# x added by ScalarE and GpSimd, token statistics in the third step, block projection and selection moved, in an attention and GRU kernel

## What is computed

```python
# x: (128, 32, 256), 128 sequences of 32 tokens; cond: (128, 256)
# 1. conditioning: 8 blocks of 4 tokens per sequence
block = x.reshape(B, 8, 4, H).sum(2)
keys = block @ Wk.T;  keys = keys / rms(keys) * rms_weight
attn = softmax(keys @ cond[1])                 # over the 8 blocks
y = layernorm(x + (attn . block) @ Wo.T) * gamma + beta
# 2. causal attention with ALiBi, 32 heads of 8, on y
x = x + attention(y) @ W_proj + b_proj
# 3. GRU over the 32 tokens, initial state cond; then a linear layer
h = gru(cond, x)
out = x + h @ (weight * scale).T + bias
```

## Time and profile before

| | |
|---|---|
| median of three runs | 433.52 us |
| profiled execution | 432.99 us, span 431.2 us |
| TensorE, matmuls | 400.7 us busy (93%) |
| TensorE, weight loads | 337.6 us (78%) |
| VectorE (DVE) | 329.7 us (76%) |
| ScalarE (ACT) | 222.1 us (52%) |
| GpSimd (POOL) | 144.9 us (34%) |
| granted TensorE clock | full throughout |

### The profile page before, as it was taken

The page is one execution under the profiler, slowest core; times in us unless marked ns, Lnnn a source line. Parts: engine busy times, 40 slices in busy tenths (PEclk is TensorE's granted clock), DMA queues, the critical chain, the costliest instruction groups (busy, mean ns, idle before and its releaser), DMA issues.

```text
span 431.2 us, 14949 instructions
## 1 busy us (share of the span) xinstructions
PE 400.7 (93%) x6216; PEld 337.6 (78%) x6216; DVE 329.7 (76%) x956; ACT 222.1 (52%) x551; POOL 144.9 (34%) x208
## 2 busy tenths in 40 slices
PE   8799889999979999898997698999999999999994
PEld 6557667887767778677785597999989999999984
DVE  3587797998998989989978565676767676767675
ACT  6354647566565665757654543444444444444331
POOL 7672474676555545456676400000000000000000
PEclk9999999999999999999999999999999999999999
DMA  7952413223232222322122000000000000000001
GB/s 288 393 209 75 124 53 100 71 83 86 66 102 82 90 81 66 111 70 82 47 64 72 3 0 2 0 27 26 24 27 24 26 24 27 27 24 26 25 26 73
DMA packets 33539, 30.46 MB, mean 71 GB/s; under 512 B 3392, under 2 KB 28608, under 8 KB 33472
## 3 DMA queue, kind: packets, MB, share of 16 engines
q1 hardware_dynamic: 33472, 29.51, 20.7%
HBM read 16.92 MB, written 8.39 MB: 59 GB/s over the span
## 4 chain that ended last, share of the span: by engine, by line
PE 62%; DVE 16%; issue 8%; POOL 7%; ACT 6%; DVEq 0%; POOLq 0%; ACTq 0%
PE ps_s L1487 7%; PE ps_t L1487 7%; PE ps_o L1487 7%; POOL sc L550 6%; PE ps_s L1560 5%; PE ps_t L1560 5%; PE ps_a L1560 4%; PE ps_m L1560 4%; PE ps_s L1386 3%; PE ps_m L1424 3%; DVE pT L1012 3%; DVE mx L1004 3%; PE ps_t L1312 3%; ACT sc L672 2%; PE ps_t L1321 2%
## 5 line engine op out<-in xcount | busy, mean ns | idle before, releaser
L550 POOL TENSOR_TENSOR sc<-masked,mx 128x512 f32<-128x512 f32 x64 | 66.3, 1057 | 71.6 <-DVE mx L1004 71.5
L672 ACT ACTIVATE sc<-sc 128x512 f32<-128x512 f32 x64 | 39.7, 629 | 23.0 <-POOL sc L550 22.6
L1012 DVE STREAM_TRANSPOSE pT<-sc 128x512 f32<-128x512 f32 x64 | 42.6, 692 | 6.5 <-ACT sc L672 6.4
L996 DVE COPY_PREDICATED masked<-kst,ps_s 128x512 f32<-128x512 int32 x64 | 44.1, 735 | 2.6 <-PE ps_s L1386 2.2
L1424 PE MATMUL ps_m<-oT,w_p 128*128 128x128 f32 x256 | 35.0, 280 | 6.8 <-ACT oT L599 6.8
L1386 PE MATMUL ps_s<-kbd,qn 32*32 32x128 f32 x2048 | 38.1, 272 | 3.4 <-issue 2.7
L1424 PEld LDWEIGHTS ps_m<-oT,w_p 128*128 128x128 f32 x256 | 32.1, 191 | 11.7 <-ACT oT L599 10.4
L790 ACT ACTIVATE zg<-ps_t,brz 128x128 f32<-128x128 f32 x64 | 20.1, 365 | 39.7 <-PE ps_t L1487 37.4
L1004 DVE TENSOR_REDUCE mx<-masked 128x16 f32<-128x512 f32 x64 | 40.4, 671 | 0.2
L1146 DVE SCALAR_TENSOR_TENSOR rg<-ps_o,vec,rg 128x128 f32<-128x128 f32 x64 | 19.5, 346 | 24.6 <-PE ps_o L1487 23.6
L1487 PEld LDWEIGHTS ps_s<-hT,w_hh 128*128 128x128 f32 x256 | 33.0, 191 | 5.1 <-DVE hT L1164 3.1
(11 more groups left out here) (168 smaller groups left out, 825.9 us busy)
## 6 DMA issues: line engine op xcount, KB each, us to landing
xf<-in_x_feat SPq DMA_DIRECT2D x8, 512.0 KB, 9.3
kbd<-kn SPq DMA_DIRECT2D x64, 64.0 KB, 2.0
v_dram<-vn SPq DMA_DIRECT2D x16, 256.0 KB, 2.8
vbd<-v_dram SPq DMA_DIRECT2D x64, 64.0 KB, 2.0
out_feat<-ost SPq DMA_DIRECT2D x16, 256.0 KB, 2.0
xg<-in_x_tok SPq DMA_DIRECT2D x24, 128.0 KB, 2.2
xg<-in_x_tok SPq DMA_DIRECT2D x2, 512.0 KB, 7.0
w_qkv<-in_wqkv SPq DMA_DIRECT2D x1, 768.0 KB, 9.5
```

Source lines behind the costliest of these rows:

```text
L550: nc.gpsimd.tensor_tensor(shifted, kept, m.unsqueeze(2).to_broadcast([P, NH // 2, S]), ALU.subtract).then_inc(sc_sub, 1)
L672: nc.scalar.activation(part, part, ACT.Exp).then_inc(sc_exp, 1)
L996: nc.vector.copy_predicated(kept, keep.unsqueeze(1).to_broadcast([P, NH // 2, S]), ps_s[:, h * 512:(h + 1) * 512].rearrange("p (h k) -> p ...
L1012: nc.vector.transpose(pT[:, cols], sc[:, p, cols]).then_inc(pt_out, 1)
```

## The change

The addition of x to the spread block projection, for groups 2 to 7, leaves VectorE. ScalarE copies the two halves from `ps_a` to `y` (`spread_out`), and GpSimd adds x to them in place (`add_tokens`), in step (g,2) ahead of `inverse_rms` and of the next tile's subtraction. VectorE takes all token statistics at the end of step (g,2), no longer half of them in step (g,3). `keep_weights` stands ahead of the masks. `select_blocks` moves on ScalarE from between the two exponentials of step (g,0) to step (g-1,3), behind the writing of xo and ahead of `normalise_tokens`. `batch_proj` moves on TensorE to the front of step (g,0), ahead of the scores, from behind the transposes of the attention output.

```diff
--- before.py
+++ after.py
@@ -225,6 +225,7 @@
         proj_hi = sem("proj_hi")
         proj_lo = sem("proj_lo")
         r_mm = sem("r_mm")
+        spread_copied = sem("spread_copied")
         z_done = sem("z_done")
         bn_done = sem("bn_done")
         pool_consts = sem("pool_consts")
@@ -573,10 +574,21 @@
                 for j, other in enumerate((block_keys(k), wqr[:, :])):
                     nc.gpsimd.tensor_tensor(junk[:, j, :], block_keys(k), other, ALU.mult).then_inc(kw_prod, 1)
 
+            def add_tokens(k):
+
+                pool.wait_ge(l_xg, DMA * (2 + GT * (k - 1)))
+                for h in range(2):
+                    pool.wait_ge(spread_copied, 2 * (k - 2) + h + 1)
+                    half = y[:, 2 * h:2 * h + 2, :].rearrange("p t e -> p (t e)")
+                    nc.gpsimd.tensor_tensor(half, half, xg[:, 2 * h:2 * h + 2, :].rearrange("p t e -> p (t e)"),
+                                            ALU.add).then_inc(z_done, 1)
+
             softmax_shift(0)
             for g in range(NG):
                 for i in range(GT):
                     n = GT * g + i
+                    if i == 2 and g + 2 < NG:
+                        add_tokens(g + 2)
                     if i == 2 and g == 2:
                         inverse_rms(3)
                     if g == NG - 2 and i > 0:
@@ -619,6 +631,13 @@
                 else:
                     act.wait_ge(r_mm, 2 * k)
                 copy_out(proj_r[0:MH, :], bank).then_inc(proj_hi, 1)
+
+            def spread_out(k, h):
+
+                act.wait_ge(yt_mm, C * k)
+                act.wait_ge(r_mm, 2 * k + h + 1)
+                copy_out(y[:, 2 * h:2 * h + 2, :].rearrange("p t e -> p (t e)"),
+                         ps_a[:, h * 512:(h + 1) * 512]).then_inc(spread_copied, 1)
 
             def cond_exp(j):
 
@@ -733,8 +752,8 @@
                     round_y(1, 0)
                     round_y(1, 1)
                 softmax_exp(n, n % 2, 0)
-                if i == 0 and 0 < g < NG - 2:
-                    select_blocks(g + 2)
+                if i == 2 and g + 2 < NG:
+                    spread_out(g + 2, 0)
                 softmax_exp(n, n % 2, 1)
                 if i == 0 and 0 < g < NG - 1:
                     round_y(g + 1, 0)
@@ -742,6 +761,8 @@
                     k_chunk(g + 1, 1)
                 if n > 0:
                     attn_out(n - 1)
+                if i == 2 and g + 2 < NG:
+                    spread_out(g + 2, 1)
                 if i == 0 and 0 < g < NG - 1:
                     round_y(g + 1, 1)
                 if i == 0 and 0 < g < NG - 2:
@@ -761,6 +782,8 @@
                     round_proj(2, proj_ps)
                 if i == 2 and not last_group:
                     v_half(g + 1, 0)
+                if i == 3 and g + 3 < NG:
+                    select_blocks(g + 3)
                 if i == 3 and g + 2 < NG:
                     normalise_tokens(g + 2)
                 if i == 3 and g + EARLY < NG:
@@ -907,7 +930,7 @@
             def add_proj_half(k, h, banks):
 
                 if h == 0:
-                    dve.wait_ge(l_xg, DMA * (k + 1 if k < 2 else 2 + GT * (k - 1)))
+                    dve.wait_ge(l_xg, DMA * (k + 1))
                     dve.wait_ge(yt_mm, C * k)
                 dve.wait_ge(r_mm, 2 * k + h + 1)
                 nc.vector.tensor_tensor(y[:, 2 * h:2 * h + 2, :].rearrange("p t e -> p (t e)"),
@@ -1093,19 +1116,16 @@
                     normalise(n - 1)
                 if (g, i) in CHAIN_END:
                     cond_normalise(2 + g // 2)
-                if norm_ahead and i == 3:
-                    some_token_stats(g + 2, 1).then_inc(bn_done, 1)
-                    mean_and_variance(g + 2)
                 if i > 0 and g < NG - 1:
                     transpose_probs(n, n % 2)
+                if (g, i) in CHAIN_END:
+                    keep_weights(2 + g // 2)
                 if n + 1 < NT:
                     softmax_mask(n + 1, (n + 1) % 2)
                 if i == 0 and g + 1 < NG:
                     rest_of_y(g + 1)
                 if (g, i) == (2, 2):
                     cond_scores(3)
-                if (g, i) in CHAIN_END:
-                    keep_weights(2 + g // 2)
                 if i == 0 or g == NG - 1:
                     transpose_probs(n, n % 2)
                 if (g, i) in CHAIN_AT:
@@ -1115,9 +1135,8 @@
                 if n + 1 < NT:
                     softmax_max(n + 1, (n + 1) % 2)
                 if norm_ahead and i == 2:
-                    add_proj(g + 2, ps_a)
-                if norm_ahead and i == 2:
-                    some_token_stats(g + 2, 0)
+                    token_stats(g + 2)
+                    mean_and_variance(g + 2)
                 if i == 1 and g + 5 < NG:
                     sums_of_products(g + 5)
                 if i == 1 and g == 2:
@@ -1495,6 +1514,9 @@
 
                 n = GT * g + i
                 last_group, norm_ahead = g + 1 == NG, g + 2 < NG
+                if i == 0 and 0 < g < NG - 2:
+                    pe.wait_ge(v_out, 2 * g + 1)
+                    batch_proj(g + 2, proj_ps_ahead)
                 if i == 1 and 0 < g < NG - 1:
                     keys(g + 1, 1)
                 if norm_ahead and i == 2:
@@ -1510,9 +1532,6 @@
                     pe.wait_ge(kw_out, EARLY)
                 if n > 0:
                     transpose_attn(n - 1)
-                if i == 0 and 0 < g < NG - 2:
-                    pe.wait_ge(v_out, 2 * g + 1)
-                    batch_proj(g + 2, proj_ps_ahead)
                 if (g, i) in CHAIN_END:
                     cond_col(2 + g // 2)
                 if i == 1 and not last_group:
```

## The result

The changed kernel takes 435.01 us (median of 20 runs, 432.87 to 436.44) against 433.52 (20 runs, 431.82 to 434.86): ratio 1.0029, 95% interval 1.0015 to 1.0043. That is slower by 1.3 us, 0.3%, at the edge of what a measurement of this kernel can tell. The forecast was 435.4, with a range of 431.0 to 437.5. Two of the 35 executions of the kernel before that stand beside root_first, sums_early, bp_back and combined took 505 and 566 us at a mean granted clock of 0.75 and 0.65, and no ratio contains them.

The account below looks back on a forecast made before the run. TensorE was taken to set the pace inside groups, with gains left at group boundaries and single waits. The terms 0.56+1.0+0.50+0.48-0.35-0.28 gave +1.91 us on the 433.52 median: 435.4 us, range 431.0 to 437.5.

Parts of the forecast that it names:

- The bound: From a group's first output projection to its fourth step TensorE sets the pace; 1.27 us off VectorE gains nothing there.
- Rival (b): VectorE is the bound: 1.27 us comes back in each of groups 2 to 5, net -2.6, 431.0 us; chance 0.17.
- The additions' price: Each new GpSimd addition of 512 columns takes 1.31 us, with 1.05 as the low end.
- Rival (a): Cheap additions on GpSimd at 1.05 us each: +0.9, 434.4 us, no measurable change; chance 0.22.
- (c): VectorE's instructions hold up GpSimd's additions, 1.7 us each: +4.5, 438 us; chance 0.10.
- Group 1: Additions delay GpSimd's subtraction, the second exponential, oT's copy and the output projection of step (1,3): +1.0 us.
- Group 2: Additions delay the root and the cond row by 1.06 us; with the boundary behind it, net +0.48.
- ScalarE's chain: From xo to the output projection at a boundary, ScalarE's own work: 4.60 us plus one selection of 0.33, 4.93.
- The boundaries 3 to 4 and 4 to 5: VectorE's earlier maximum leaves only ScalarE's own 4.93 us of 5.28: -0.35 at the first, -0.28 at the second.
- The block projection in front: Two matmuls no longer fill the wait for oT's copy: +0.56 at 0 to 1, +0.50 at 1 to 2, later nothing.
- The sum: All terms, 0.56+1.0+0.50+0.48-0.35-0.28, make +1.91 us on the whole kernel; +0.9 with cheap additions.
- Rival (d): Seven TensorE gaps without a releaser, up to 0.91 us, fall elsewhere: 0.9 either way, 434.5 to 436.3; chance 0.06.

Follow-up runs that it names:

- root_first: The changed kernel with the reciprocal root ahead of the additions on GpSimd in step (2,2): 433.64 us, ratio 1.0003.
- sums_early: The changed kernel with group 7's block sums moved on GpSimd from the end of step (1,1) to the start of (1,0): 432.50 us, ratio 0.9982.
- bp_back: The changed kernel with the block projection back behind the transposes of the attention output: 432.76 us, ratio 0.9981.
- combined: The changed kernel with the edits of bp_back, sums_early and root_first together: 431.10 us, ratio 0.9951.
- dve_pad: The changed kernel with two useless VectorE instructions added in step (g,2) of groups 2 to 5, 1.27 us a group: 436.74 us, ratio 1.0062.
- no_add: The changed kernel with each GpSimd addition cut from 512 columns to 4, which changes the output: 432.68 us, ratio 0.9972.
- after_again: The changed kernel unedited, run again for a second profile: 434.17 us, ratio 1.0010.
- moves_alone: The kernel before with only block projection, selection and kept weights moved; additions and statistics stay on VectorE: 434.81 us, ratio 1.0028.
- root_cs: root_first with the three-column product of scores and root moved from VectorE to GpSimd, right behind the root: 433.87 us, ratio 0.9999.
- best: combined with root_cs's product on GpSimd and the block chain's mean on ScalarE: 430.12 us, ratio 0.9915.

## Why the prediction was right, point by point

**The bound.** Right. Group 3 keeps 18.98 us from first to fourth output projection against 18.92, with 1.27 us less on VectorE; TensorE sets the pace inside a group. dve_pad adds that VectorE is only 0.7 us behind in step 2 of groups 3 and 4. Rival (b) falls with both.

**The additions' price.** 1.29 us by the median of twelve, where 1.31 was taken from the nearest row in kind and 1.05 was the low end. Rival (a) falls, and so does (c): none of the twelve took over 1.31. The estimate of 1.12 from the Trainium skill ("GPSIMD Engine Reference", section 3) is low by 0.17 here.

**Group 1.** +1.0 forecast, +0.85 in its middle and 0.08 more at its end. The queue on GpSimd came as described: the subtraction starts 3.94 us behind the output projection of step (1,2), where the prediction had 91.84-87.79 = 4.05. The wait that it named as the last was the wrong one. It put the late exponential and the copy of oT first and called VectorE's normalising late "by less"; TensorE waits 0.73 us for the normalised output ahead of the transposes and not at all ahead of the output projection, as the values fill the time of the copy (95.32+0.37 = 95.69). That both came to about the same is luck. sums_early and no_add show that the additions in GpSimd's queue are the cause.

**Group 2.** The wait ahead of the cond row was put at 1.06 and is 1.04, but the net +0.48 came out as +0.10. Of the missing 0.38, 0.10 lies in the middle of the group, which grew by 0.96 and not 1.06. The mis-sized term is ScalarE's chain: 4.60+0.33=4.93 us from xo to the output projection, measured 4.65. The 4.60 was read at the boundary 5 to 6, where two exponentials took 1.30 us and TensorE's transposes of y have a wait in them; at 3 to 4 the pair takes 1.14, and the selection, overlapped with the writing of xo, adds 0.22 (151.28 to 151.50) and not 0.33. A floor read at one place held a wait of that place.

**The boundaries 3 to 4 and 4 to 5.** The same term: -0.35 and -0.28 forecast, -0.63 and about -0.54 measured (5.76 and, in after_again, 5.77). moves_alone, with 6.56 and 6.04, shows that the first comes with the additions and statistics, as forecast, and that half of the second comes with the moves. At 5 to 6, put at 0, it is -0.17 against the first profile.

**The block projection in front.** +0.56 and +0.50 forecast; +0.54 and +0.63 measured, of which 0.55 each goes with bp_back and stands alone in moves_alone. The idle ahead of the output projection is 0.47 us, not 0.9: the 0.86 goes from start to start, and 0.38 of it are the transposes. Nothing at the later boundaries, as forecast.

**The sum.** 0.54+0.85+0.63+0.10-0.57-0.49-0.17 = +0.9 (the fifth and sixth terms are groups 3 and 4 with their boundaries, 25.31 to 24.74 and, by after_again, 25.24 to 24.75), where +1.9 was forecast; with the second profiles of both kernels it is +0.5. The medians say +1.3 (0.7 to 1.9). The missing 0.4 is as much as the changed kernel's profiles are behind at the start, 0.35 to 0.71 us, where the edit changes nothing on TensorE; that it is that is argued, not shown. So it is in part luck that the forecast of 435.4 lies 0.4 us from the measured 435.01: the places came to half of the sum, which is also the +0.9 of rival (a), though the additions weren't cheap. The direction and the places were right, the gain at the boundaries was too small by half a microsecond in all, and in group 2 by 0.4.

**What was overlooked.** The text said that no VectorE instruction beside the additions has two SBUF inputs. The product of the block chain has; it escaped in the changed kernel only because it waited for the root anyway, and showed at once in root_first. The rule was read for GpSimd as the one that is held up, not for VectorE.

**Rival (d).** The gaps without a releaser do move, with the same kernel; one of 0.70 us sits in group 4 of one profile of the changed kernel and not of the other. With the clock of 0.79 at 242 to 250 us they make up 2.05 of the 3.4 us between the two spans. The kernel before has six of them in its waits, not seven. They don't fall just anywhere: one ahead of the last 32 score matmuls of step (5,1) stands in each of the 13 profiles, and it is always near 0.25, 0.55, 0.82 or 1.10 us long. What decides whether and how long is open, and it wasn't tried.

## What to carry to other kernels

Taking work off an engine that isn't the bound of a stage gains nothing in that stage: 1.27 us off VectorE left the middle of group 3 as long as it was and gained 0.6 us at the boundary, where its maximum had been late. Where the engine that takes it over has a queue, price what stands behind it, and look for an idle stretch earlier in that queue. Here the block sums moved sooner, the root and its product ahead of the additions, the mean on ScalarE and the block projection put back turned a loss of 1.3 us into a gain of 3.7, of which about one lies where no edit reaches. An instruction that fills a wait is free where it stands and costs its full length where TensorE has no idle time: 0.55 us at the first two boundaries, nothing at the later ones. When a group's length repeats to 0.1 us and the total only to 1, judge an edit by the group.

## What the runs showed of the hardware

A small VectorE instruction can be held for as long as a large GpSimd one runs: 1.12 us instead of 0.16 for a product of three columns with two SBUF inputs beside an addition, 0.94 instead of 0.17 for a multiply-add of three columns with a single one beside a subtraction, each ending within 0.02 us of GpSimd's. For the product root_cs shows the cause, as the wait goes with the instruction; for the multiply-add it is read from the equal ends and from best. Masks (0.74 us), maxima (two in 1.27) and statistics (two in 0.75) ran beside the additions at their usual length. The Trainium skill, "SBUF — State Buffer", under "Who interferes with whom", states it: a VectorE instruction with two SBUF inputs contends with a GpSimd instruction that reads SBUF, and one in a two-port mode, which `tensor_scalar` can enter, contends with GpSimd as well; whoever issues first has the port pair for its whole instruction. Both rows agree; that the multiply-add ran in such a mode no run here shows.
